# A mixture-of-experts layer before and after a gated attention: the order of VectorE's work between two experts, and how the experts' token lists are summed on TensorE

## The reference

```
x = x + 0.5 * moe(layernorm(x))
x = x + linear_attention(layernorm(x))      # 16 heads of 64, gated scan over 4096 tokens
x = x + 0.5 * moe(layernorm(x))             # the same weights again

def moe(x):                                 # E = 8 experts, top 2, capacity 1228 a expert
    logits = x @ router_w + router_b
    probs, experts = softmax(top_k(logits, 2)), indices
    pos    = running count of a pick within its expert (first choices of all tokens first)
    rows   = the first 1228 picks of an expert, gathered
    h, g   = rows @ w_c_fc[e] + b, rows @ w_gate[e] + b        # 256 -> 1024
    o      = silu(h * g) @ w_c_proj[e] + b                      # 1024 -> 256
    return sum over the two picks of probs * o[expert, pos]
```

## Time and profile before

| | |
|---|---|
| median of 3 runs | 2220.95 us (2217.06 to 2223.34) |
| the profiled execution | 2220.27 us, of it span from first to last instruction 2218.5 us |
| TensorE busy | 2020.2 us, 91% of the span |
| VectorE, ScalarE, GpSimd busy | 61%, 55%, 16% |
| mean granted TensorE clock | 0.957 of 2.4 GHz |

### The profile page before, as it was taken

One profiled execution on the slowest core, in us unless ns is written; L12 is line 12 of the kernel. 1 busy time (PEld: TensorE's weight loads), 2 busy tenths in 40 slices (PEclk: granted clock), 3 DMA queues, 4 the chain that ended last, 5 costly groups with the idle time before them and its releaser, 6 DMA issues.

```text
span 2218.5 us, 36527 instructions
## 1 busy us (share of the span) xinstructions
PE 2020.2 (91%) x13365; PEld 1687.6 (76%) x13368; DVE 1353.4 (61%) x2723; ACT 1210.6 (55%) x1958; POOL 360.0 (16%) x560
## 2 busy tenths in 40 slices
PE   5499999999996999999999999994999999999990
PEld 2388878887885788888888887862888888887880
DVE  6756655565556648576575856658555555665663
ACT  2366655665454746565564655633655664765540
POOL 0111101110102202112020200001201101110335
PEclk9599999999998999999999999996999999999995
DMA  6113221222122000000000000031222221232225
GB/s 211 63 54 97 93 90 44 86 95 87 45 96 64 20 1 21 9 12 15 6 20 6 16 1 1 1 114 33 90 65 71 80 76 49 89 95 86 71 66 158
DMA packets 84174, 133.10 MB, mean 60 GB/s; under 512 B 10200, under 2 KB 65824, under 8 KB 84064
## 3 DMA queue, kind: packets, MB, share of 16 engines
q1 hardware_dynamic: 69472, 94.67, 12.6%
q0 software_dynamic: 14592, 36.93, 6.0%
HBM read 98.84 MB, written 32.70 MB: 59 GB/s over the span
## 4 chain that ended last, share of the span: by engine, by line
PE 77%; PEld 7%; DVE 6%; ACT 3%; issue 3%; POOL 2%; DMA 1%; PEldq 1%; SPq 0%; DVEq 0%; POOLq 0%
PE bank L626 29%; PE bank L697 12%; PE bank L643 8%; PE bank L790 4%; PE bank L645 4%; PEld bank L626 4%; PE bank L773 3%; PE bank L723 3%; PE bank L778 3%; PE bank L745 3%; PEld bank L643 2%; PE bank L758 2%; POOL halves L460 2%; PE bank L732 1%; PE bank L565 1%
## 5 line engine op out<-in xcount | busy, mean ns | idle before, releaser
L626 PE MATMUL bank<-halves 128*128 128x512 f32 (+2 forms) x3744 | 773.5, 367 | 24.6 <-DVE halves L1242 24.6
L626 PEld LDWEIGHTS bank<-halves 128*128 128x128 f32 x3744 | 651.2, 191 | 133.0 <-issue 27.7
L895 ACT ACTIVATE temp<-bank,bias_now 128x512 f32<-128x512 f32 (+1 forms) x312 | 200.1, 641 | 369.9 <-PE bank L626 369.6
L643 PE MATMUL bank<-halves 128*128 128x512 f32 (+1 forms) x1096 | 387.4, 397 | 3.1 <-issue 3.1
L1261 DVE SCALAR_TENSOR_TENSOR temp<-bank,bias_fc,temp 128x512 f32<-128x512 f32 (+1 forms) x312 | 216.0, 692 | 215.4 <-ACT temp L895 211.9
L436 POOL DMA_INDIRECT wide<-normed,spare x160 | 162.9, 1018 | 1030.2 <-PE bank L607 844.0
L645 PE MATMUL bank<-halves 128*128 128x256 f32 (+1 forms) x1096 | 306.4, 280 | 0.0
L697 PE MATMUL bank<-halves 128*128 128x512 f32 x1152 | 285.8, 399 | 3.6 <-DVE halves L1398 2.3
L1268 DVE TENSOR_TENSOR halves<-temp,halves 128x512 fp32r<-128x512 f32 (+1 forms) x312 | 198.0, 635 | 125.4 <-ACT halves L844 122.3
L697 PEld LDWEIGHTS bank<-halves 128*128 128x128 f32 x1152 | 212.0, 189 | 51.5 <-issue 2.7
L643 PEld LDWEIGHTS bank<-halves 128*128 128x128 f32 (+1 forms) x1096 | 203.2, 185 | 55.0 <-issue 5.9
(11 more groups left out here) (186 smaller groups left out, 2281.8 us busy)
## 6 DMA issues: line engine op xcount, KB each, us to landing
expert_out<-rows SPq DMA_DIRECT2D x144, 128.0 KB, 1.7
wide<-in_L_ffn_w_c_fc SPq DMA_DIRECT2D x16, 1024.0 KB, 5.6
wide<-in_L_ffn_w_gate SPq DMA_DIRECT2D x16, 1024.0 KB, 7.6
wide<-in_L_ffn_w_c_proj SPq DMA_DIRECT2D x16, 1024.0 KB, 5.4
normed<-wide SPq DMA_DIRECT2D x8, 1024.0 KB, 4.8
x<-in_L_attn_x SPq DMA_DIRECT2D x4, 1024.0 KB, 7.0
out_x<-x SPq DMA_DIRECT2D x32, 128.0 KB, 2.3
wide<-normed,spare POOLq DMA_INDIRECT x160, 2.8
```

Source lines behind the costliest of these rows:

```text
L626: m = pe.matmul(bank[at + b][:, 0:w], a[:, kc, j * P:(j + 1) * P], v[:, kc, 0:w], start=(i == 0), stop=(i == len(ps) - 1))
L643: pe.matmul(bank[4 + t % 2][0:m, :], s_hi[buf][:, j, o:o + m], pr[:, j, :], start=(j == 0), stop=False, skip_group_check=True)
L895: nc.scalar.activation(g_sb[b][:, 0:w], bank[2 + b][:, 0:w], ACT.Identity, bias=bias_now[:, j:j + 1]).then_inc(g_copied, 1)
```

## The change

Three things are done.

1. VectorE's order between two experts. The eight pieces of the next weights are done three ahead of output tile 4, three ahead of tile 5 and two ahead of tile 6, and the turned rows ahead of tile 6. Before, they were two each ahead of tiles 4 to 7, and the rows ahead of tile 7.
2. The token lists. The tile number is no longer multiplied into the moving side. The matmuls write the marks themselves into up to six blocks of 80 columns of a PSUM bank: block 0 takes the own number, block b + 1 takes the mark of each pick whose tile number has bit b set. VectorE then weighs the blocks with 1, 128, 256, ... 2048 and adds them. The third VectorE instruction for each 8 tiles goes, and TensorE does 120 matmuls in place of 64 in a layer, and one more that clears the six blocks. `by_list` holds `[own number | mark]`, and the ScalarE copy reads and writes in it.
3. Seven more constants are set in `set_constants` in each layer: `nothing` (480 zeros in bfloat16) and the six one-column weights.

```
+DIGITS = 1 + (TILES - 1).bit_length()
 ...
 def make_lists():                                     # TensorE
+    digits = bank[1][:, 0:DIGITS * LISTS].rearrange("p (a n) -> p a n", n=LISTS)
+    pe.matmul(bank[1][:, 0:DIGITS * LISTS], ones, nothing, start=True, stop=False, skip_group_check=True)
     for j in range(PICKS):
         if j % MARKS == 0:
             pe.wait_ge(rows_marked, n)
-            pe.wait_ge(tiles_marked, n)
+            pe.wait_ge(lists_marked, n)
             pe.wait_ge(own_marked, n)
-        m = pe.matmul(bank[0][:, 0:2 * LISTS], by_row[:, j, :], by_list[:, j, :], ...)
+        own_and_list = by_list[:, j, :].rearrange("p (a n) -> p a n", n=LISTS)
+        bits = [b + 1 for b in range(DIGITS - 1) if j % TILES >> b & 1]
+        if not bits:
+            m = pe.matmul(digits[:, 0, :], by_row[:, j, :], own_and_list[:, 0, :], start=False, ...)
+            continue
+        m = pe.matmul(digits[:, 0:bits[0] + 1:bits[0], :], by_row[:, j, :], own_and_list, start=False, ...)
+        rest = bits[1:]
+        while rest:
+            step = rest[1] - rest[0] if len(rest) > 1 else 1
+            run = [b for k, b in enumerate(rest) if b == rest[0] + k * step]
+            m = pe.matmul(digits[:, run[0]:run[-1] + 1:step, :], by_row[:, j, :],
+                          own_and_list[:, 1:2, :].to_broadcast([P, len(run), LISTS]), start=False, ...)
+            rest = rest[len(run):]
 ...
 def set_constants():                                  # VectorE
     steps.after(v.memset(ones, 1.0))
+    steps.after(v.memset(nothing, 0.0))
+    for b in range(DIGITS):
+        steps.after(v.memset(worth[:, b:b + 1], float(P << b - 1) if b else 1.0))
 ...
 for n in range(PICKS // MARKS):                       # VectorE, make_lists
-    v.tensor_tensor(here[:, at, :], ..., ALU.is_equal).then_inc(lists_marked, 1)
+    v.tensor_tensor(by_list[:, at, LISTS:2 * LISTS], ..., ALU.is_equal).then_inc(lists_marked, 1)
     v.tensor_tensor(by_row[:, at, :], ..., ALU.is_equal).then_inc(rows_marked, 1)
-    dve.wait_ge(lists_marked, r * PICKS // MARKS + n + 1)
-    v.tensor_tensor(by_list[:, at, 0:LISTS], here[:, at, :], ..., ALU.mult).then_inc(tiles_marked, 1)
 ...
 dve.wait_ge(listed, r + 1)                            # VectorE, route
-steps.after(v.tensor_copy(owners, bank[0][:, LISTS:2 * LISTS]))
-v.scalar_tensor_tensor(tokens, bank[0][:, 0:LISTS], float(P), owners, ...).then_inc(tokens_made, 1)
+steps.after(v.tensor_tensor(weighed, bank[1][...], worth.unsqueeze(2).to_broadcast([P, DIGITS, LISTS]), ALU.mult))
+steps.after(v.tensor_reduce(named, weighed.rearrange("p a n -> p n a"), AX_X, ALU.add))
+v.tensor_copy(tokens, named).then_inc(tokens_made, 1)
 ...
 for t in range(4, Y_TILES):                           # VectorE, expert
-    if not last and t < 8:
-        split_fc(u * 8 + 8, 2 * (t - 4))
-        split_fc(u * 8 + 8, 2 * (t - 4) + 1)
-    if not last and t == 7:
+    if not last and t < 7:
+        for k in range(3 * (t - 4), min(3 * (t - 3), 8)):
+            split_fc(u * 8 + 8, k)
+    if not last and t == 6:
         turned(r, e + 1, 0)
     ...
     y_out(t)
```

More of the change, by code:

```diff
@@ L183, in macaron @@
         total = room(2336, E)
-        owners = room(2344, LISTS)
+        named = room(2344, LISTS)
+        weighed = room(3520, DIGITS, LISTS)
+        nothing = room(4000, DIGITS * LISTS // 2).bitcast(BF16)
+        worth = room(4240, DIGITS)
         by_row = part(route_space, 12288, PICKS * P // 2).bitcast(BF16).rearrange("p (j n) -> p j n", n=P)
@@ L188, in macaron @@
         own = part(spare, LISTS, 1)
-        here = part(route_space, 21504, PICKS * LISTS // 2).bitcast(BF16).rearrange("p (j n) -> p j n", n=LISTS)
         row16, list16 = (room(2424 + PICKS // 2 * n, PICKS // 2).bitcast(BF16) for n in range(2))
@@ L239, in macaron @@
         index_made = sem("index_made")
-        lists_known, rows_marked, lists_marked, tiles_marked, own_marked = (
-            sem("lists_known"), sem("rows_marked"), sem("lists_marked"), sem("tiles_marked"), sem("own_marked"))
+        lists_known, rows_marked, lists_marked, own_marked = (
+            sem("lists_known"), sem("rows_marked"), sem("lists_marked"), sem("own_marked"))
         listed, tokens_made = sem("listed"), sem("tokens_made")
@@ L551, in make_lists @@
                             pe.wait_ge(rows_marked, n)
-                            pe.wait_ge(tiles_marked, n)
+                            pe.wait_ge(lists_marked, n)
                             pe.wait_ge(own_marked, n)
-                        m = pe.matmul(bank[0][:, 0:2 * LISTS], by_row[:, j, :], by_list[:, j, :],
-                                      start=(j == 0), stop=(j == PICKS - 1))
+                        stop = j == PICKS - 1
+                        own_and_list = by_list[:, j, :].rearrange("p (a n) -> p a n", n=LISTS)
+                        bits = [b + 1 for b in range(DIGITS - 1) if j % TILES >> b & 1]
+                        if not bits:
+                            m = pe.matmul(digits[:, 0, :], by_row[:, j, :], own_and_list[:, 0, :],
+                                          start=False, stop=stop, skip_group_check=True)
+                            continue
+                        m = pe.matmul(digits[:, 0:bits[0] + 1:bits[0], :], by_row[:, j, :], own_and_list,
+                                      start=False, stop=stop, skip_group_check=True)
+                        rest = bits[1:]
[3 more added lines that the diff above has]
+                            m = pe.matmul(digits[:, run[0]:run[-1] + 1:step, :], by_row[:, j, :],
+                                          own_and_list[:, 1:2, :].to_broadcast([P, len(run), LISTS]),
+                                          start=False, stop=stop, skip_group_check=True)
+                            rest = rest[len(run):]
                     m.then_inc(listed, 1)
@@ L864, in route @@
                     act.wait_ge(lists_marked, r * PICKS // MARKS + n + 1)
-                    nc.scalar.activation(by_list[:, at, LISTS:2 * LISTS], here[:, at, :], ACT.Copy,
+                    nc.scalar.activation(by_list[:, at, 0:LISTS], by_list[:, at, LISTS:2 * LISTS], ACT.Copy,
                                          scale=own).then_inc(own_marked, 1)
@@ L1153, in make_lists @@
                     at = slice(n * MARKS, (n + 1) * MARKS)
-                    first = n * MARKS % TILES
-                    v.tensor_tensor(here[:, at, :], index16[:, 0:LISTS].unsqueeze(1).to_broadcast([P, MARKS, LISTS]),
+                    v.tensor_tensor(by_list[:, at, LISTS:2 * LISTS], index16[:, 0:LISTS].unsqueeze(1).to_broadcast([P, MARKS, LISTS]),
                                     spread(list16[:, at], LISTS), ALU.is_equal).then_inc(lists_marked, 1)
@@ L1158, in make_lists @@
                                     spread(row16[:, at], P), ALU.is_equal).then_inc(rows_marked, 1)
-                    dve.wait_ge(lists_marked, r * PICKS // MARKS + n + 1)
-                    v.tensor_tensor(by_list[:, at, 0:LISTS], here[:, at, :], spread(index16[:, first:first + MARKS], LISTS),
-                                    ALU.mult).then_inc(tiles_marked, 1)
             def normalise_rows(s):
@@ L1197, in route @@
                 dve.wait_ge(listed, r + 1)
-                steps.after(v.tensor_copy(owners, bank[0][:, LISTS:2 * LISTS]))
-                v.scalar_tensor_tensor(tokens, bank[0][:, 0:LISTS], float(P), owners,
-                                       ALU.mult, ALU.add).then_inc(tokens_made, 1)
+                steps.after(v.tensor_tensor(weighed, bank[1][:, 0:DIGITS * LISTS].rearrange("p (a n) -> p a n", n=LISTS),
+                                            worth.unsqueeze(2).to_broadcast([P, DIGITS, LISTS]), ALU.mult))
+                steps.after(v.tensor_reduce(named, weighed.rearrange("p a n -> p n a"), AX_X, ALU.add))
+                v.tensor_copy(tokens, named).then_inc(tokens_made, 1)
             def settle_weights(r):
```

## The result

The changed kernel takes 2190.22 us (median of 4 runs, 2188.31 to 2190.54) against 2221.16 us before (4 runs): a ratio of 0.9858, 95% interval 0.9846 to 0.987. The profiled execution took 2190.38 us, its span is 2188.6 us, 29.9 less than before. TensorE is busy 92% of it, and the mean granted clock is 0.969 (0.957 before).

The account below looks back on a forecast made before the run. TensorE, busy 91% of the span, was taken as the bound. Experts 21.1 us (11.9 + 9.2) plus lists 7.1 give 28.2 off 2220.3: 2192.1, stated as 2192.5 us for the median; range 2186 to 2204.

Parts of the forecast that it names:

- Gap: TensorE's idle time at five expert changes ending with tile 6: 3.55 us falls to 1.17, gaining 11.9 us in all.
- VectorE's steps, worked out piece by piece: Between experts, VectorE finishes the turned rows at 230.8, before TensorE ends tile 6 at 231.1, 0.3 us in hand.
- Clock: First 48 matmuls after the five gaps: the granted clock no longer falls, about 11.17 us each, gaining 9.2 us.
- 1.17 is nearer to 0.77 than to 3.55: At the five gaps: no clock loss shows after 0.77 us, so the whole 9.2 us was taken, 0 the other end.
- Behind tile 7: Four expert changes ending with tile 7, 0.77 us idle each: gain taken as 0, bounds 0 and 1.5 us.
- Lists: Token lists in routing: bank read 5.8 us sooner a layer with the clock risen, 4.2 at clock 0.50.
- The evaluation: VectorE's multiply, strided reduction and cast after the bank read: 1.87 us in place of 0.52, +1.35 a layer.
- Constants: Zeros and six one-column fills on VectorE at layer 0's start: cost 1.75 us, all on the path; hidden in layer 1.
- A clock that stays low in the lists: Rival, token lists: granted clock stays at 0.50, each layer gains 1.6 us less, 2195.7 us; chance 0.22.
- A clock that still falls in the five places: Rival, expert starts behind tile 6: clock still falls, 9.2 us comes back, 2201.7 us; chance 0.12.
- Matmuls that don't pipeline: Rival, token lists: each matmul costs 0.334 us alone, bank read 25.8 us later, twice: 2244 us, slower; chance 0.04.
- The PSUM Cachelines rule: List matmuls' output: non-contiguous PSUM patterns slow matmuls a lot; expected not to bite, with 80 adjacent values in a block.

Follow-up runs that it names:

- The run with one drain: Kernel with layer 0's constants set behind the last normalised rows, plus TensorE's group 2 question nested in the group 1 question, one drain for two: 2187.18 us.
- The run with gaps of 2.35: Changed kernel with the turned rows' low parts ahead of output tile 7 again, weight pieces by threes as changed: 2202.99 us, ratio 0.992.
- the light batch: List batches ordered 1, 2, 3, 5, 6, 7, 0, 4: on the changed kernel with later constants 2186.24 us; with one drain and side-by-side digits too, 2187.25 us.

## Why the prediction was right

**Gap.** I gave 3.55 - 1.17 = 2.38 each, 11.9 in all; measured 12.3. The floor of 1.17, built from one drain and the place behind tile 7, is 1.09. The run with one drain shows that it is made of just that: 0.71 is left, about what the place behind tile 7 has, and 0.38 goes with the drain and its branch. VectorE's steps, worked out piece by piece, ended 0.3 us ahead of tile 6; measured 229.19 against tile 6's last matmul at 229.24 + 0.28 = 229.52. Where group 2 has rows no gap came: `up` starts there 0.16 us before the last matmul's modelled end, as before.

**Clock.** Expected 9.2, found 8.9. The step "1.17 is nearer to 0.77 than to 3.55" was the weakest: it was an interpolation between two values. The run with gaps of 2.35 shows that the middle already loses most of it (four of five), so a forecast of a gap of 2 us by the same step could have been wrong by most of the 9 us. That 1.17 fell on the good side was partly luck; nothing in the trace of before lay between 0.77 and 3.55 at these places.

**Behind tile 7.** Taken as 0 although the profile named VectorE for it; 0.3 for four. Reading the 24.6 us of the earlier trace rows as all VectorE's would have promised 3.1 us there.

**Lists.** Forecast 5.8 a layer with the clock risen, 4.2 without; measured 6.1 and 5.8. The clock rose in the third batch in layer 0 and in the fourth in layer 1, which was the likeliest case and not the sure one. The evaluation was priced at +1.35 and took 1.38 and 1.39, the reduction 0.97 for 0.95, the multiply 0.66 for 0.65.

**Constants.** Forecast 1.75, measured 1.25; the term was oversized in both pieces. The zeros took 0.26 and not 0.48, since they were issued as half as many words, and the small fills came every 0.125 us rather than 0.2. That they lie on the path was right: taking all of layer 0's constants off it brought the first expert 1.8 us sooner.

**What the sum did not have.** One slip is in the sum itself: 2192.1 and the 0.7 by which the median lies above the profiled execution are 2192.8, not 2192.5; nothing hangs on it. The clock in the rest of the program gave +0.5 net out of parts of up to 2.3 each. The forecast of 2192.5 is 2.3 above the median; 1.1 of that are the terms above (0.4 gap, 0.3 behind tile 7, 0.3 lists, 0.5 constants, less 0.3 of clock and 0.1 of evaluation), the rest is this remainder and the scatter.

**The rivals.** A clock that stays low in the lists: refuted by the stretch of 74.3 to 82.5. A clock that still falls in the five places: refuted 45 times in 45. Matmuls that don't pipeline: refuted by 0.036 us a matmul of 80 columns. The PSUM Cachelines rule of the Trainium skill ("Advanced Engine Details and Errata"), read strictly, would have made the jumping output slow; the traces don't show that for runs of 80 adjacent values: at full clock the matmuls of 160 columns into two blocks, neighbouring or not, follow each other at about 0.07 us, and two of 80 columns into single blocks take 2 x 0.036.

## What to carry to other kernels

An engine's program order can hold back what another engine needs behind a wait for that other engine's output: list what is ready when, and put first what releases the bottleneck. Price an idle stretch of TensorE together with the matmuls behind it: here a gap of 3.55 us cost 5.3, the gap of 1.1 nothing more than itself. And a wait named in the profile isn't all curable, since the control instructions beside it (here 0.4 us a drain with its branch) are a floor that a place without the wait shows.

## What the runs showed that I had not expected

- A matmul of 80 columns with its own 128x128 weight load costs 0.036 us when 36 stand in a row at full clock, against 0.033 for the columns alone.
- At one and the same gap of 2.35 us the clock fell in four places of five, and behind one idle stretch of 2.03 us in three profiles of twelve.
- Where the constants were taken off the start of layer 0, the read of the lists' bank in layer 0 came 0.36 us later after the first mark, in four profiles of four (after allowing for the 0.54 of the light batch in two of them), for no cause that a row shows.
- A strided write on VectorE cost here about as much as a strided read: 0.66 to 1.02 us for 480 values 24 bytes apart, against 0.65 to 0.97 us for reading them 320 bytes apart.
- A fill of 480 bfloat16 zeros took 0.26 us, issued as 240 words, half of what a fill of 512 ones takes (0.48).
- Nesting one question on TensorE in the other removed 0.38 us from one way through the code and put 0.23 us on another.
